# Mamba: the input product of state 5 of 16 by ScalarE's scaling and TensorE's transposes into banks 0 and 1

## The reference, cut to what matters

```python
delta = softplus(dt @ dtp_w.T + dtp_b)          # one step size per token and channel
A = -exp(A_log)                                 # 256 channels x 16 states
def step(h, inp):
    u_t, d_t, b_t, c_t = inp
    dA = exp(d_t[:, :, None] * A)
    h = h * dA + (d_t * u_t)[:, :, None] * b_t[:, None, :]
    y = einsum('bdn,bn->bd', h, c_t)
    return (h, y)
```

## Time and profile before

| what | value |
|---|---|
| device time, median of 3 runs | 2616.86 us (2615.24 to 2616.86) |
| profiled execution | 2614.2 us, span in the trace 2612.1 us |
| granted TensorE clock, mean over the span | 0.962 |
| busy over the span | PE 85%, DVE 86%, ACT 73%, POOL 84% |
| Mamba stages in the trace | about 534 to 2090 us |

### The profile page before, as it was taken

How to read it: one execution, slowest core, us unless ns; L and a number is a source line. 1 busy time by engine, 2 the same in 40 slices (tenths; PEclk the granted TensorE clock), 3 DMA queues, 4 the chain that set the end, 5 groups by cost and what they waited for, 6 DMA issues and landing times.

```text
span 2612.1 us, 48904 instructions
## 1 busy us (share of the span) xinstructions
PE 2227.8 (85%) x15840; PEld 1908.7 (73%) x15840; DVE 2240.6 (86%) x3430; ACT 1895.3 (73%) x3628; POOL 2198.4 (84%) x1402
## 2 busy tenths in 40 slices
PE   4899999668888898888888888888988768999992
PEld 3799999446776777776776766766766647999992
DVE  8766666789999999999999999999999887666666
ACT  4355555389999989999999999999999543555551
POOL 3677777379999999999999999999999936777772
PEclk8999999889999999999999999999999978999996
DMA  7011112533333333333333333333333240111126
GB/s 249 21 48 49 49 50 50 144 94 105 110 103 104 107 106 102 107 107 101 111 101 103 112 100 105 111 107 104 106 107 107 85 161 24 50 49 49 49 49 211
DMA packets 156821, 248.73 MB, mean 95 GB/s; under 512 B 22082, under 2 KB 66018, under 8 KB 155874
## 3 DMA queue, kind: packets, MB, share of 16 engines
q1 hardware_dynamic: 137568, 202.79, 26.1%
q0 software_dynamic: 18208, 37.26, 5.3%
q10 hardware_dynamic: 866, 6.43, 0.6%
HBM read 213.10 MB, written 33.29 MB: 94 GB/s over the span
## 4 chain that ended last, share of the span: by engine, by line
PE 37%; POOL 19%; DVE 15%; issue 14%; ACT 10%; DMA 4%; ACTq 0%; DVEq 0%; POOLq 0%; SPq 0%
PE bank L1351 10%; POOL buf L548 8%; DVE buf L917 7%; PE bank L1547 6%; PE bank L1372 6%; PE bank L1422 4%; POOL token_outputs L497 4%; POOL buf L487 4%; PE bank L1522 3%; PE bank L1332 3%; ACT over L1164 3%; DMA buf<-state_rows 2%; ACT scaled L1197 2%; DVE buf L904 2%; POOL buf L535 2%
## 5 line engine op out<-in xcount | busy, mean ns | idle before, releaser
L548 POOL TENSOR_TENSOR buf<-buf 128x1024 f32<-128x1024 f32 x512 | 1199.9, 2374 | 32.4 <-PE bank L1547 27.0
L917 DVE TENSOR_TENSOR_SCAN buf<-over,bank 128x512 f32<-128x512 f32 x832 | 953.8, 1200 | 4.9 <-PE bank L1522 2.7
L1164 ACT ACTIVATE over<-wgu,negA 128x510 f32<-128x510 f32 x832 | 541.5, 709 | 40.3 <-DVE buf L917 28.8
L1547 PE MATMUL bank<-id_sb,buf 128*128 128x128 f32 x4096 | 515.8, 279 | 6.8 <-POOL buf L548 6.8
L1547 PEld LDWEIGHTS bank<-id_sb,buf 128*128 128x128 f32 x4096 | 478.2, 144 | 57.2 <-issue 46.6
L1351 PE MATMUL bank<-parts 128*128 128x256 f32 x3408 | 447.6, 288 | 17.3 <-DVE buf L767 9.2
L1351 PEld LDWEIGHTS bank<-parts 128*128 128x128 f32 x3408 | 420.7, 193 | 36.7 <-issue 36.7
L1197 ACT ACTIVATE scaled<-wd_sb,I 128x256 f32<-128x256 f32 x896 | 377.3, 497 | 22.6 <-PE bank L1522 22.5
L497 POOL DMA_INDIRECT token_outputs<-buf,slot_out x284 | 299.5, 1055 | 87.9 <-issue 84.0
L487 POOL DMA_INDIRECT buf<-token_rows,slot_token x284 | 284.5, 1002 | 95.4 <-issue 82.5
L1522 PE MATMUL bank<-id_sb,scaled 128*128 128x128 f32 x1792 | 256.0, 280 | 88.3 <-ACT scaled L1197 38.2
(11 more groups left out here) (170 smaller groups left out, 3061.6 us busy)
## 6 DMA issues: line engine op xcount, KB each, us to landing
buf<-state_rows SPq DMA_DIRECT2D x608, 256.0 KB, 3.2
token_rows<-buf SPq DMA_DIRECT2D x32, 256.0 KB, 2.3
wd_sb<-token_outputs SPq DMA_DIRECT2D x16, 512.0 KB, 4.0
buf<-token_outputs SPq DMA_DIRECT2D x16, 512.0 KB, 4.8
buf<-token_rows,slot_token POOLq DMA_INDIRECT x284, 2.5
token_outputs<-buf,slot_out POOLq DMA_INDIRECT x284
out<-X SPq DMA_DIRECT2D x16, 256.0 KB, 3.6
wgu<-wgT ACTq DMA_DIRECT2D x1, 2048.0 KB, 9.1
```

What stands on the lines that cost most here:

```text
L548: pool.tensor_tensor(hC[:, b, :].rearrange("p (c w) -> p c w", c=C), hs[:, b, :].rearrange("p (c w) -> p c w", c=C), Cs[:, b, :].unsqueeze ...
L917: V.tensor_tensor_scan(hs[:, b, w], dA[:, b, c, :, :].rearrange("p s t -> p (s t)"), source, 0.0, ALU.mult, ALU.add).then_inc(s[f"scan_don ...
L1164: ins = A.activation(dA[:, n % R, c, :, 1:], delta[r][:, c * W:(c + 1) * W].rearrange("p (s t) -> p s t", s=S)[:, :, 1:], ACT.Exp, scale=n ...
L1547: ins = M.matmul(bank[4 + q // 2][:, at:at + P], hC[:, n % R, c * W + q * P:c * W + (q + 1) * P], id_sb[:, :], is_transpose=True, start=Fa ...
```

## The change

State 5 moves from the second way (spread and VectorE's product) to the third (ScalarE's scaling and TensorE's transposes), but its transposes go into banks 0 and 1 instead of 2 and 3, since the banks 2 and 3 are taken by states 4 and 6. ScalarE's scalings of states 5, 6 and 8 take places 1.5, 3.0 and 4.5. `turn_back` waits for the scan of state 3, which read banks 0 and 1 last.

```diff
 POOL_UNITS = (3, 9, 15)
-TURNED_UNITS = (2, 4, 6, 8, 10, 12, 14)
-SCALE_AT = {0.5: (0, 4), 1.5: (0, 6), 3.0: (0, 8), 6.0: (0, 10), 9.0: (0, 12), 12.0: (0, 14), 15.5: (1, 2)}
+TURNED_UNITS = (2, 4, 5, 6, 8, 10, 12, 14)
+TURNED_LOW = (5,)
+SCALE_AT = {0.5: (0, 4), 1.5: (0, 5), 3.0: (0, 6), 4.5: (0, 8), 6.0: (0, 10), 9.0: (0, 12), 12.0: (0, 14), 15.5: (1, 2)}
...
         def turned_bank(n, c):
 
+            if n in TURNED_LOW:
+                return bank[c]
             last = (vector_before(0, n) - 1) % 2
             return B_bank[last if c else 1 - last]
...
                 pe.wait_ge(s["scaled_done"], turned_before(u, n) + 1)
-                last = max((m for m in TURNED_UNITS if m < n), default=TURNED_UNITS[-1] - NS)
-                wait(pe, s["scan_done1"], u * NS + last + 1)
+                low = n in TURNED_LOW
+                last = max((m for m in TURNED_UNITS if m < n and m not in TURNED_LOW), default=TURNED_UNITS[-1] - NS)
+                if not low:
+                    wait(pe, s["scan_done1"], u * NS + last + 1)
                 for c in range(C):
-                    wait(pe, s["mul_done"], 2 * (vector_before(u, n) - 1 + c))
+                    if low:
+                        wait(pe, s[f"scan_done{c}"], u * NS + n - 1)
+                    else:
+                        wait(pe, s["mul_done"], 2 * (vector_before(u, n) - 1 + c))
```

## The result

The changed kernel takes 2661.97 us (median of 4 runs, 2656.24 to 2662.76), the kernel before, run beside it, 2616.11 (2615.24 to 2616.86). The ratio is 1.0171, with a 95% interval of 1.0153 to 1.0188: 46 us slower. The forecast was 2637, with a range of 2598 to 2660. The sign was right, the size was not, and the time lies just outside the range. The profiled execution took 2662.76 us, its span is 2661.0.

What follows compares the result with a forecast made beforehand. No engine alone was the bound; a ring of ScalarE and TensorE had almost no air in stage A. 16 stages A at 0.9 and 15 B at 0.4 added 20.4 us: 2637 us, 8 in 10 between 2598 and 2660.

Steps and rivals of the forecast that it cites:

- VectorE's relief: VectorE loses state 5's two products, 1.36 us a stage; counted as nothing, upper bound 1.43 us in a pair.
- the rival of VectorE: VectorE was the bound and its saved work comes through: 2595 us, or 2606 at half; chance 0.27.
- ScalarE's way: Added scalings, 1.6 us a stage, delay state 12's scaling and transposes: 0.9 us in A, nothing in B.
- TensorE's order: State 5's transposes ahead of the skip delay `project_x` and GpSimd's state 4: 0.4 us in B, about 0.65 in A.
- ScalarE's term in a stage A: Scaling 12 comes 1.6 us later, less waits used up behind it: 0.9 us left, bounds 0 and 1.6.
- both ways added: Rival: ScalarE's and TensorE's delays add up, A costing 1.6 us and B 0.8 to 0.95: 2657 us; chance 0.15.
- the delay through `project_x`: TensorE's later `project_x`, 0.8 us in B, about 0.65 in A; one rival had it reach ScalarE's `split_hi`.

Runs made afterwards that it cites:

- e9: Kernel before, with VectorE's two products of state 5 cut from 512 to 16 columns and no other engine given work: 2616.55 us, ratio 1.0007.
- e6: Changed kernel, with ScalarE's copy of B's columns at place 7.5 instead of 8.0 and state 5's transposes behind the skip: 2648.22 us.
- e1: Changed kernel, with one of state 8's four scalings kept, so one scaling is added instead of four: 2629.98 us.
- e5: Changed kernel, with ScalarE's copy of B's columns at place 7.5 instead of 8.0, ahead of state 9's decays: 2645.25 us.
- e4: Kernel before, with only ScalarE's added work: state 8 scaled twice, at places 3.0 and 4.5: 2655.74 us, ratio 1.0166.
- e3: Changed kernel, with 14 idle transposes on TensorE ahead of its wait for the copy of B's columns: 2647.88 us.
- e2: Changed kernel, with state 5's transposes behind the skip on TensorE instead of ahead of it: 2661.18 us.
- e8: Changed kernel, with one of state 8's four scalings kept and state 5's transposes behind the skip: 2621.47 us, ratio 1.0028.
- e7: Kernel before, with ScalarE's copy of B's columns at place 7.5 instead of 8.0: 2638.25 us, ratio 1.0099.

## Why the prediction was wrong

**What held.**

- VectorE's relief is worth nothing (e9), and the place that takes it is `split_lo`: 0.41 us before, 1.63 after. So the rival of VectorE, at 0.27 the strongest, does not happen; ScalarE, with 92% of the pair in use, could not take the work for nothing.
- State 5's transposes wait for the scan of state 3 (1.17 and 0.44 us), and the skip begins 4.73 us behind `project_z` (1146.70 to 1151.43) where it began 1.83 behind in the earlier trace rows.
- Where the clock does not fall, the terms hold: ScalarE's way costs 0.75 us in A and 0.05 in B (e6), against 0.9 and nothing; TensorE's order 0.58 and 0.69 (e1), against 0.65 and 0.4 (bounds 0 and 0.8); in A one lies beside the other and not on top of it. Both together make 1.2 us in a pair (e5), against 1.3.
- ScalarE has no bracket from `split_hi` to the scaling of state 12, and its waits before state 9's decays in B are gone (the L1177 of the changed kernel, 600 to 1980):

```profile
L1177 ACT ACTIVATE bank<-wgu,negA 128x512 f32<-128x512 f32 x164 | 105.5, 674 | 0.0
```

**The step that failed** is ScalarE's term in a stage A: "Left: 0.9 us in a stage A. Its bounds are 0 and 1.6." A stage A grew by 2.06 us, above the upper bound, and e4 shows that ScalarE's work alone does it. What the term left out is TensorE's clock: the window of a pair was read at full granted clock, every matmul behind the delay was put down at the length that it had, and a fall of the clock was put at nothing without a reason. I let ScalarE's 1.6 us meet TensorE at one place, the scaling of state 12, and took from them the waits that lie behind it. But ScalarE meets TensorE earlier, at the copy of B's columns, and there TensorE was already waiting 1.09 us in A. That row was in the trace, and I did not read it, since I had followed TensorE only from state 12 on. The wait grew by 1.08, the clock fell behind it, the next matmuls took 1.7 us longer, and the spread of state 11, VectorE's product and the second half of state 12's transposes came late through them. With VectorE late as well, the spread of state 13 goes on waiting its 0.42 us, which the term had taken off. That is why the term is larger than the work that was added: I had taken 1.6 us as the most that 1.6 us of work can cost. The place alone is not the cause: where the copy's wait is filled (e3) or shortened (e5), the clock still falls in many stages behind the wait for state 12's scaling, the place that the prediction had, and only the pairs without any fall come to the forecast.

In B the forecast gave ScalarE nothing ("with a bound of 0.95") and TensorE's order 0.4. B grew by 0.86, and it is again ScalarE's together with the clock (e4: 0.80; e2: no change; 0.05 without a fall, e6). In eight of the 14 stages B the same place does it; timeline of the stage B after:

```profile
1215.13 0.47 PE L1468 MATMUL bank<-BCs,dtp_high 104*128 104x512 f32 x1 [1.74 <-ACT I L1183]
1216.59 1.91 PE L1530 MATMUL bank<-id_sb,scaled 128*128 128x128 f32 x8
```

In the other six the wait is as long, the transposes behind it take 1.04 us, and the clock falls behind state 12's wait.

**The rival that comes nearest in number**, both ways added, 2657, is not what happened: e2 takes the one way out and nothing comes back. Its conditions did not hold either: in A `split_hi` begins 2.77 us behind the norm before and 2.76 after, so the delay through `project_x` does not reach it, and at full clock A does not cost 1.6 (e5: 0.75). That its number is near is chance.

**What stays open.** With e8, where one extra scaling of 0.4 us is left, B is still 0.43 us longer than before, and the whole is 1.0028 (1.0016 to 1.0039); how much of it is that scaling, how much the transposes of state 5 and how much its 18 falls of the clock, no run tells apart. How the 46 us split is an estimate: 1.2 us in 15.5 pairs, 19 us, for the two delays at full clock, close to the 20 of the forecast, and the rest, 27 us, for the clock. It takes e5's pairs without a fall for those of the changed kernel, which has none, and rests on e7 for the copy's place costing nothing by itself. Why the clock falls in one stage and holds in the next, behind waits of the same length, no run shows. No variant here beats the kernel before.

## What to carry to other kernels

When work is added to an engine, list every place behind it where another engine waits for that engine, in order of time, and start with the first that already has a wait: here a copy of 0.2 us came ahead of the large step that the prediction looked at. A wait on TensorE that gets longer may cost more than its length, so where the engine already stands still for a microsecond, the upper bound is not the work added, and the granted clock of the stretch behind it is to be read. Where the clock falls in some stages only, compare those in which it holds: that tells its share from the rest without another run. An engine's relief is worth something only if what it waits for next is not what gets the work.

## What the runs showed of the hardware

That the clock falls inside a loop that keeps TensorE busy 88% of the time was not expected. In the stages A shown, a wait of 1.09 us before the matmuls of the step size left the clock at 1.00, and one of 2.17 us was followed by 0.50, with eight transposes at 1.79 and 1.91 us (after, and e4) instead of 1.04. In the stage B a wait of 1.74 us was followed by transposes of 1.91. With 14 transposes in the wait they took 1.04. That wait is not the only place: the kernel before has 12 falls in 28 stages, and 10 with the wait filled. Nor does the length of one wait decide: behind waits of 1.74 us in stages B of the changed kernel the clock fell in eight and held in six, and behind waits of 2.37 us before state 12's transposes in stages A of e5 it fell in seven and held in four. What the falls cost can be read from pairs with the same instructions: 97.6 us without one and 98.5 to 100.9 with falls behind that wait in A (e5).
